# The start and the last tile of a fused adaLN block with linear attention and routed experts: first modulation rows, tile 0 and weight splits reordered

## The reference, cut to what matters

```python
mod = (_silu(L0_c) @ L0_wmod).reshape(L0_c.shape[0], 6, 1, -1)
sa, ca, ga, sb, cb, gb = (mod[:, 0], mod[:, 1], mod[:, 2], mod[:, 3], mod[:, 4], mod[:, 5])
h = _layernorm(x, axis=-1) * (1 + ca) + sa
x = x + ga * _L0_attn_ref(h, ...)      # linear attention: relu(q), relu(k), v, key-value sums, projection
h = _layernorm(x, axis=-1) * (1 + cb) + sb
x = x + gb * _L0_ffn_ref(h, ...)       # two shared and 8 routed experts (top 2), INTER = 352
```

## Time and profile before

| | us |
|---|---|
| median of 3 runs | 1216.98 (1216.12 to 1217.58) |
| profiled execution: its time | 1217.89 |
| profiled execution: span, first to last instruction | 1216.1 |
| TensorE busy in the span | 1189.8 (98%) |
| VectorE busy | 805.9 (66%) |
| GpSimd busy | 506.3 (42%) |
| ScalarE busy | 417.7 (34%) |
| TensorE in the chain that ended last | 90% |

### The profile page before, as it was taken

One profiled execution on the slowest core, in us unless ns is written; L12 is line 12 of the kernel. 1 busy time (PEld: TensorE's weight loads), 2 busy tenths in 40 slices (PEclk: granted clock), 3 DMA queues, 4 the chain that ended last, 5 costly groups with the idle time before them and its releaser, 6 DMA issues.

```text
span 1216.1 us, 25326 instructions
## 1 busy us (share of the span) xinstructions
PE 1189.8 (98%) x9054; PEld 776.8 (64%) x9054; DVE 805.9 (66%) x1578; ACT 417.7 (34%) x873; POOL 506.3 (42%) x409
## 2 busy tenths in 40 slices
PE   7999999999999999999999999999999999999996
PEld 2646666666666666767777777656666666666663
DVE  5647778878776777655857754266666666666665
ACT  4424444445443432333323323222222222222221
POOL 2212566656564554222112112345445554455543
PEclk9999999999999999999999999999999999999998
DMA  7816597998788978745434535579787897779783
GB/s 238 228 40 168 125 250 192 214 234 212 182 222 185 229 209 197 173 99 120 122 87 104 137 85 117 111 150 135 132 141 140 131 132 139 138 135 136 133 127 45
DMA packets 253255, 185.27 MB, mean 152 GB/s; under 512 B 186496, under 2 KB 198784, under 8 KB 253132
## 3 DMA queue, kind: packets, MB, share of 16 engines
q1 hardware_dynamic: 217368, 114.40, 42.1%
q0 software_dynamic: 20512, 45.62, 22.4%
q10 hardware_dynamic: 15256, 23.62, 6.7%
HBM read 87.07 MB, written 52.75 MB: 115 GB/s over the span
## 4 chain that ended last, share of the span: by engine, by line
PE 90%; DVE 2%; issue 2%; DMA 2%; POOL 1%; ACT 1%; SPq 0%; ACTq 0%; POOLq 0%; DVEq 0%
PE ps_o L87 7%; PE ps_o L89 7%; PE ps_o L88 7%; PE ps_vs L87 6%; PE ps_vs L88 6%; PE ps_vs L89 6%; PE ps_kh L87 4%; PE ps_vh L87 4%; PE ps_vh L88 4%; PE ps_vh L89 4%; PE ps_kh L88 4%; PE ps_kh L89 4%; PE ps_qh L87 4%; PE ps_qh L89 4%; PE ps_qh L88 4%
## 5 line engine op out<-in xcount | busy, mean ns | idle before, releaser
L444 POOL DMA_INDIRECT out<-y,slot_row x71 | 139.3, 1963 | 190.3 <-DVE y L882 138.7
L89 PE MATMUL ps_o<-w_all,xt 128*128 x568 | 177.5, 313 | 0.0
L88 PE MATMUL ps_o<-w_all,xt 128*128 x568 | 177.5, 313 | 0.0
L87 PE MATMUL ps_o<-w_all,xt 128*128 x568 | 177.5, 312 | 0.0
L874 DVE SCALAR_TENSOR_TENSOR gate_row<-gate_rows,batch_weight,gate_row 128x512 f32<-128x512 f32 x213 | 158.9, 746 | 2.5
L368 POOL DMA_INDIRECT out<-s_sum,row_no x32 | 53.8, 1680 | 197.6 <-DVE s_sum L623 192.0
L1133 ACT ACTIVATE at<-ps_y 128x384 f16<-128x384 f32 x71 | 34.8, 491 | 250.7 <-PE ps_y L1353 247.1
L330 POOL TENSOR_TENSOR h<-cen,rows_f 128x512 f32<-128x512 f32 x32 | 40.6, 1270 | 130.6 <-ACT cen L901 115.4
L89 PE MATMUL ps_qh<-ht,wqkv 128*128 128x128 f16 x512 | 87.4, 219 | 0.0
L88 PE MATMUL ps_qh<-ht,wqkv 128*128 128x128 f16 x512 | 87.4, 219 | 0.0
L87 PE MATMUL ps_qh<-ht,wqkv 128*128 128x128 f16 x512 | 87.4, 219 | 0.0
(11 more groups left out here) (251 smaller groups left out, 3341.2 us busy)
## 6 DMA issues: line engine op xcount, KB each, us to landing
w_stage<-in_w_d ACTq DMA_DIRECT2D x64, 176.0 KB
xb<-in_x SPq DMA_DIRECT2D x32, 256.0 KB, 3.7
xr<-in_x SPq DMA_DIRECT2D x32, 256.0 KB, 4.0
out<-x SPq DMA_DIRECT2D x32, 256.0 KB, 3.6
h_d<-hl SPq DMA_DIRECT2D x32, 256.0 KB, 2.5
h2t_d<-h2t SPq DMA_DIRECT2D x32, 256.0 KB, 3.5
s_ht<-h2t_d SPq DMA_DIRECT2D x32, 256.0 KB, 3.6
sstage<-in_sh_flat SPq DMA_DIRECT2D x32, 136.0 KB, 3.6
```

What stands on the lines that cost most here:

```text
L87: nc.tensor.matmul(out, lh, rh, start=first, stop=False, skip_group_check=True)
L88: nc.tensor.matmul(out, lh, rl, start=False, stop=False, skip_group_check=True)
L89: return nc.tensor.matmul(out, ll, rh, start=False, stop=last, skip_group_check=True)
L444: pool.indirect_dma_start(m.out, bass.IndirectOffsetOnAxis(ap=m.slot_row[:, t:t + 1], axis=0), m.y[:, t % Y_RING, :], None, compute_op=ALU ...
```

## The change

At the start:
- sct_rep now repeats all four items, 32 columns each, so that the 16 products give the first two rows of all items; the scale row (CA) is made ahead of the shift row. modulate(0) and modulate(1) are gone. The rows are copied to modrows, the store to memory takes one partition of each 32, and the row of item 0 is spread over the partitions by a product with one row of ones into two PSUM banks.
- Tile 0 is centred and scaled in one instruction before the rows are there, multiplied and shifted by VectorE out of PSUM, and turned by four TensorE transposes; two half tiles are copied and split (turned_high, turned_low). Its DMA transpose is gone. The copies of the rows to rows_f, for the tiles behind it, are made by ScalarE later.
- The splits of pieces 5 and 6: ScalarE scales the staged piece in place (scale_stage), GpSimd subtracts the high part. All stage loads are issued by SyncE. The staging ring has 8 places, and the first loads are mixed with those of wmod. The run-in of VectorE and ScalarE is written out by hand. TensorE waits for the splits of tile 0's products one by one.

At the experts: the two halves of at lie in separate buffers, e_high(0) waits for less and stands ahead of first_gate_row(0), and e_multiply(1) stands ahead of the gate rows. At the last tile e_turn stands inside e_down of the tile before, and VectorE's order is changed to fit.

```diff
-CONSTS = 5
-SPLITS_FIRST = {-2: (4,), -1: (6,), 0: (10, 11)}
-SPLITS_LAST = {-2: (5,), -1: (7, 8, 9)}
+ONE_READY, IDENT_READY, V_READY, HEADS_READY = 1, 4, 6, 11
+POOL_SPLITS = (5, 6)
+PE_TURNED = 1
+COPIES = P // B
...
+        if 1 <= k < 3:
+            sp.dma_start(m.stage[:, k - 1, :], m.pieces[k - 1][0]).then_inc(m.stage_loaded[k - 1], 16)
+    load_x(1)
+    for n in range(2, 2 * KC):
         sp.dma_start(m.stage[:, n, :], m.pieces[n][0]).then_inc(m.stage_loaded[n], 16)
-    load_x(1)
     load_x(2)
+    for n in range(2 * KC, 3 * KC):
+        sp.wait_ge(m.stage_lo, n - STAGE_RING + 1)
+        sp.dma_start(m.stage[:, n % STAGE_RING, :], m.pieces[n][0]).then_inc(m.stage_loaded[n % STAGE_RING], 16)
...
+    def split_low(n):
+        dst = m.pieces[n][1]
+        pool.wait_ge(m.stage_scaled, POOL_SPLITS.index(n) + 1)
+        pool.wait_ge(m.stage_hi, n + 1)
+        pool.tensor_tensor(dst[:, 1, :], m.stage[:, n % STAGE_RING, :], dst[:, 0, :], ALU.subtract).then_inc(m.stage_pool, 1)
...
+        if s == -1:
+            split_low(POOL_SPLITS[0])
         shift(s + 2)
+        if s == -1:
+            split_low(POOL_SPLITS[1])
...
+    v.wait_ge(m.silu_done, 1)
+    for k in range(KC):
+        v.tensor_copy(m.sct_rep[:, k, :].rearrange("p (b n) -> p b n", b=B), m.sct[:, k, :].unsqueeze(2).to_broadcast([P, B, COPIES])).then_inc(m.rep_done, 1)
+    stats(0)
+    v.wait_ge(m.rstd_done, 1)
+    v.tensor_scalar(m.cen[:, 0, :], m.xb[:, 0, :], m.mv[:, 0, 0:1], m.rstd[:, 0, :], ALU.subtract, ALU.mult).then_inc(m.cen_done, 1)
+    split_low(0)
+    split_low(1)
+    v.wait_ge(m.bc_done, 1)
+    v.tensor_scalar(m.modrows[:, C:2 * C], m.ps_o[:, 1, :], 1.0, None, ALU.add).then_inc(m.row_done, 1)
+    stats(1)
+    v.wait_ge(m.spread_done, 1)
+    v.tensor_tensor(m.h[:, 0, :], m.cen[:, 0, :], m.ps_row[CA], ALU.mult).then_inc(m.scaled, 1)
+    v.wait_ge(m.spread_done, 2)
+    v.wait_ge(m.scaled, 1)
+    v.tensor_tensor(m.h[:, 0, :], m.h[:, 0, :], m.ps_row[SA], ALU.add).then_inc(m.h_done, 1)
+    centre(1)
+    turned_low(0)
+    turned_low(1)
+    for n in (2, 3, 4, 7):
+        split_low(n)
+    h_low(1)
+    for n in (8, 9):
+        split_low(n)
+    k_low(0)
+    for n in (10, 11):
+        split_low(n)
+    v_low(0)
+    stats(2)
+    for s in range(TILES + TAIL):
...
     for t in range(1, SLOT_TILES + 1):
-        e_low(t - 1)
-        gate_rows_of(t - 1, 1)
+        last = t == SLOT_TILES - 1
+        if t < SLOT_TILES:
+            e_low(t - 1)
+        if t == 1:
+            e_multiply(t)
+        if t < SLOT_TILES:
+            gate_rows_of(t - 1, 1)
         gate_rows_of(t - 1, 2)
-        if t < SLOT_TILES:
+        if last:
+            gate_rows_of(t - 1, 3)
+        if 1 < t < SLOT_TILES:
             e_multiply(t)
-        gate_rows_of(t - 1, 3)
+        if last:
+            gate_rows_of(t, 1)
+            e_low(t)
+        else:
+            gate_rows_of(t - 1, 3)
         e_out(t - 1)
...
+    for n in range(3):
         split_high(n)
+    act.wait_ge(m.bc_done, 2)
+    act.activation(m.modrows[:, 0:C], m.ps_o[:, 0, :], ACT.Copy).then_inc(m.row_done, 1)
+    for n in range(3, 6):
+        split_high(n)
+    scale_stage(POOL_SPLITS[0])
+    act.wait_ge(m.h_done, 1)
+    act.activation(m.rows_f[:, 0, SA, :], m.ps_row[SA], ACT.Copy).then_inc(m.row0_done, 1)
+    turned_high(0)
+    turned_high(1)
+    scale(1)
+    split_high(6)
+    scale_stage(POOL_SPLITS[1])
+    split_high(7)
+    h_high(1)
+    split_high(8)
+    split_high(9)
+    k_high(0)
+    split_high(10)
+    split_high(11)
+    act.wait_ge(m.cen_done, 2)
+    act.activation(m.rows_f[:, 0, CA, :], m.ps_row[CA], ACT.Copy).then_inc(m.row0_done, 1)
+    v_high(0)
+    for s in range(TILES + TAIL):
...
     e_silu(0)
-    first_gate_row(0)
     for t in range(1, SLOT_TILES):
         e_high(t - 1)
+        if t == 1:
+            e_silu(t)
+            first_gate_row(0)
         first_gate_row(t)
-        e_silu(t)
+        if t > 1:
+            e_silu(t)
...
-        for r in (0, 1):
+        for r in (CA, SA):
             mm = nc.tensor.matmul(m.ps_o[:, r, :], m.sct_rep[:, k, :], m.wmod[:, k, r * C:(r + 1) * C], start=k == 0, stop=k == KC - 1)
             if k == KC - 1:
                 mm.then_inc(m.bc_done, 1)
-    modulate(0)
-    pe.wait_ge(m.row0_done, 2)
-    modulate(1)
+    pe.wait_ge(m.consts, IDENT_READY)
+    pe.wait_ge(m.row_done, 2)
+    for r in (CA, SA):
+        nc.tensor.matmul(m.ps_row[r], m.one[0:1, :], m.modrows[0:1, r * C:(r + 1) * C], start=True, stop=True).then_inc(m.spread_done, 1)
+    pe.wait_ge(m.h_done, 1)
+    for k in range(KC):
+        mm = nc.tensor.transpose(m.ps_first[k // 2][:, k % 2, :], m.h[:, 0, k * P:(k + 1) * P], m.ident[:, :])
+        if k % 2:
+            mm.then_inc(m.first_turned, 1)
...
-    def e_down(t, expert):
+    def e_down(t, expert, turn_within=False):
         pe.wait_ge(m.e_at_lo, t + 1)
         at_least(pe, m.ey_ready, t)
         for k in range(IT):
+            if turn_within and k == 1:
+                e_turn(t + 1)
...
-        e_down(t - 1, expert)
+        e_down(t - 1, expert, t == SLOT_TILES - 1)
         expert = following
-    e_turn(SLOT_TILES - 1)
     e_down(SLOT_TILES - 1, expert)
```

More of the change, by code:

```diff
@@ L157, in turn_h @@
     def turn_h(i):
-        if tile(i):
+        if tile(i) and i >= PE_TURNED:
             sp.wait_ge(m.h_lo, i + 1)
@@ L977, in split_high, with scale_stage @@
         act.activation(m.pieces[n][1][:, 0, :], m.stage[:, n % STAGE_RING, :], ACT.Copy, scale=SCALE).then_inc(m.stage_hi, 1)
+    def scale_stage(n):
+        act.wait_ge(m.stage_hi, n + 1)
+        act.activation(m.stage[:, n % STAGE_RING, :], m.stage[:, n % STAGE_RING, :], ACT.Copy, scale=SCALE).then_inc(m.stage_scaled, 1)
     def activate(q):
```

180 lines of the change are left out of this document (82 added, 98 removed).

## The result

The changed kernel takes 1221.89 us (median of 8, 1220.25 to 1223.07) against 1217.49 us (8, 1215.74 to 1219.89): ratio 1.0028, 95% interval 1.0015 to 1.0041. The forecast was 1216.5, "within 0.2%", with a range up to 1219.6. It was wrong, and on the side of its rival (b), beyond (b)'s own 1220.4. The profiled execution of the changed kernel took 1220.25 (span 1218.5), that of the kernel before 1217.89 (span 1216.1). The first is the fastest of its eight, 1.6 us under its median, and the second is 0.4 over its own: of the 4.4 us between the medians, 2.0 are in neither profile. The granted clock of the eight says where to look: it is 0.994 in the two fastest, 0.991 and 0.992 in the two slowest.

A forecast was written before the change was run, and what follows sets the result against it. TensorE, busy 98% of the span, was taken as the bound; +1.5 (start) - 1.76 (first expert tile) - 0.25 (end) = -0.5 us from the 1216.98 median gave 1216.5, range 1213.2 to 1219.6.

The forecast's parts named there:

- rival (b): Start: stretched wmod issues (+2.05 us) lengthen TensorE's second gap, and its clock falls (1.8 us); 1220.4 us, chance 0.12.
- Part 1: First rows and tile 0: without the DMA transpose, tile 0's key products start at 20.8 instead of 25.41, 4.6 us earlier.
- Part 2: Splits behind tile 0's start: GpSimd's work slows VectorE, stats(2) at 30.3; tile 1 starts at 32.5 instead of 35.82.
- Part 3: Steps 0 and 1: later h_high(2) and six DMA issues delay v_low(1); two TensorE waits, tile 2 1.5 us later.
- Later steps keep that distance: Behind tile 2: the 1.5 us delay stays as it is, TensorE having no gap there.
- the six issues: ScalarE's DMA issues queued behind h_high(2), ahead of sh_high(0), q_high(0), k_high(1) and v_high(1), in Part 3.
- that of 2.51 did not: Mid-kernel, ahead of 405.69: TensorE's idle time of 2.51 us in the kernel before did not leave its clock low.
- Part 4: First expert tile: at(0) no longer waits for the gate rows, TensorE's 1.60 us stop goes; -1.76 us.
- Part 5: End: the last tile's turn moves into the previous tile's down products; -0.25 us, bounds -0.3 and 0.
- The sum: Whole kernel: +1.5 at tile 2, -1.76 at the experts, -0.25 at the end, giving -0.5 us.

The follow-up runs named there:

- nopool: Changed kernel with splits 5 and 6 back on VectorE instead of GpSimd, and without ScalarE's two extra scalings; 1221.6 us, ratio 1.0024.
- sp_issue: Changed kernel with the first four wmod loads issued by SyncE, behind the turning of tile 2, instead of by ScalarE; 1222.1 us, ratio 1.0025.
- small_first: Changed kernel with step 0's four wmod issues on ScalarE cut to 64 columns each, the rest in steps 1 and 2; 1217.4 us, ratio 0.9995.
- late: Changed kernel with ScalarE's eight wmod loads issued in steps 1 and 2 instead of 0 and 1; 1213.59 us, ratio 0.9966.
- sh_early: Changed kernel with step 1's small weight load (136 KB) issued one step earlier, ahead of the wmod loads; 1219.7 us, ratio 1.0013.
- fill: Changed kernel with nine and eight extra unused products of 128x512 in TensorE's two waits of step 1; 1220.9 us, ratio 1.0020.
- sh_store: Changed kernel with step 1's small weight load issued in step 0 and SyncE's row-store wait moved behind the turning of tile 4; 1221.1 us, ratio 1.0024.
- experts_only: Kernel before with only the expert parts of the change (e_high, e_low, e_down and their orders); 1215.57 us, ratio 0.9982.
- start_only: Changed kernel with the expert parts of the kernel before, so only the start of the change; 1223.49 us, ratio 1.0040.
- order: Changed kernel with VectorE's statistics and centring of tile 2 taken ahead of the low parts of k(0) and v(0); 1219.0 us, ratio 1.0009.

## Why the forecast was wrong, by its own steps

**Part 1** held: key products of tile 0 at 19.82, forecast 20.8, no turning by DMA ahead. In another profiled execution of the same start they came at 21.59; TensorE's clock in the products before decides it (8.73 and 10.18 us for the sixteen), so the forecast lies between the two, and which of them the profile caught is luck.

**Part 2** held in kind and was a little too dear. stats(2) started at 28.58, forecast 30.3, bounds 28.1 and 30.9; the sums of tile 0 were done at 31.0, forecast 32.5. That two splits on GpSimd buy next to nothing is shown by nopool. The rule of the Trainium skill (SBUF - State Buffer, Who interferes with whom) is borne out in kind: 4.53 us for four splits, where three alone took 2.00. In full it was too dear: it gave stats(2) at 30.6.

**Part 3, first half**, was right almost to the number: from h_high(2), 32.98, to the sums of tile 1, 43.41, it is 10.43 us, with 10.55 forecast (34.5 to 45.05); the two waits are 2.18 and 2.04, with 2.5 and 2.2 forecast. sp_issue and small_first confirm the cause. Tile 2 came 0.70 later than before (44.91 against 44.21; the 44.37 of the forecast is a later product of the tile), 1.5 forecast. That the two numbers are near is in part luck: with stats(2) 1.7 us sooner, Part 3's own arithmetic puts tile 2 at -0.2. The other 0.9 us come from what the forecast had at nothing, turned rows that land only at 44.86 and sums at the lower clock.

**The step that failed** is the sentence "Later steps keep that distance, as TensorE is without a gap there". It looked at TensorE alone. I had shown in step 1 that the other engines had only 0.5 us to spare, and did not ask the same question of step 2. There a second chain runs, over the small weight load, q_high(1), centre(4), scale(4), shift(4), h_high(4) to v_low(2), and all of it hangs on transfers: the changed kernel puts the turning of tile 2 (34.36), the first wmod loads (34.01 to 36.8), the small load (36.34) and the row store (37.14) into 3 us. The 0.70 us at tile 2 became 2.51 at tile 3. Step 1 needed the same question: the turned rows of tile 2 hung on the same transfers. Part 3 had counted the six issues for the time that they hold ScalarE, and gave no price to the 2 MB that they start; the row with the answer was at hand, since in the kernel before ScalarE already stands still for such a load one step on:

```profile
53.17 0.43 ACT L931 ACTIVATE sh<-sstage 128x272 f16<-128x272 f32 x1 [2.98 <-DMA sstage<-in_sh_flat]
```

late, sp_issue, small_first and sh_early show it: without the bytes the small load is in time (44.02, no wait for it) and so are the turned rows; with the bytes there, and the small load issued sooner, the turned rows of tile 2 are what comes late.

**Rival (b)** named the right engine and the wrong size. The issues did not stretch (2.77 us). The clock fell all the same (the forecast's own sign of a slower result, products of tile 2 that stand 0.43 apart, came true), behind two waits of 2.18 and 2.04 us, which the rival had thought too short; and in the changed kernel it cost next to nothing there, as fill shows, because the next wait took it up (in sh_store, where no wait followed, the key products of tile 2 took 2.5 us more at it). Behind 408.18, where no long wait follows, the same kind of fall cost 1.7 us at first and 1.4 in the end, most of what the experts gained; the forecast had it at nothing. My reading of the earlier trace rows ("that of 2.51 did not") was one execution of a thing that goes either way: of the fourteen profiled executions without extra products there, seven show the fall and seven don't.

**Parts 4 and 5** held together by the medians: experts_only gained 2.0 us, forecast 1.76 + 0.25. In the profile of the changed kernel Part 4 came out whole (-1.76) and Part 5 at half: the last scatter moved by -0.12 (forecast -0.25, bounds -0.3 and 0). The span ends 0.35 us later behind that scatter than before, which no part of the forecast had; in experts_only it is 0.28, and why stays open.

**The sum** was -0.5; the profiled executions show +2.36. Of the 2.9 us between, 1.0 is tile 3 (2.51 in place of 1.5), 1.4 the clock in mid-kernel, and the rest, some 0.5, lies at the end, 0.35 of it behind the last scatter. The rest up to the +4.4 of the medians isn't in the two profiles. The lower clocks of the other runs (0.991 to 0.993) point to further stretches at 1.2 GHz; in start_only and nopool, the key products of tile 2 took 5.1 us at such a clock. That is argued from those profiles, not shown for the changed kernel.

## To carry to other kernels

When a change brings work forward, follow every engine until all of them are back on their old schedule, not just until TensorE is busy again; the order in which large loads, transposes and small loads were issued was part of the old schedule. Count a DMA issue twice, for the engine that it holds and for the bytes that it starts, and look at which small load a strictly ordered engine must wait for behind them. Here the change to the start was worth having only with the bulk loads moved by one step as well: the whole change is 0.9966 with it, 1.0028 without, and its expert parts alone are 0.9982. By the medians the start is then worth 2.0 us (1213.59 against 1215.57); the intervals of these two ratios just overlap.

## What the runs showed of the hardware

- TensorE's granted clock can fall to half behind two waits of 2.0 to 2.2 us (44 to 48 us: 0.63), and behind a single one of 2.5 us (0.59 in 408 to 412) or not: with the same wait the profiles of the kernel before, order and small_first show 1.00 there. Ten products that nobody uses kept it at 1.00 in both runs that had them, and the rest of those kernels took 1.1 and 1.9 us less.
- A load of 136 KB whose median is 3.6 us to landing took 11.6 with 2 MB of loads and one DMA transpose issued around it; a transpose whose median is 3.8 took 10.5, issued 0.35 us behind the first of these loads. Issued ahead of them it took 3.1 (sp_issue) and 4.5 (kernel before), with 128 KB in their place 3.2 (small_first).
- Throughput says little of how busy the DMA engines are: 206 GB/s at a busy share of 1.15, 394 at 1.04.
- Four DMA issues on ScalarE took 2.33 us for 32 KB each and 2.77 for 512 KB each, beside SyncE's transpose in both.
